# Inverse denominators of a linear attention: spread by ScalarE copies and turned by TensorE, in place of a masked VectorE spread and fp32 products

## The reference, cut to what matters

```python
kv = jnp.einsum('bshd,bshe->bhde', k, v)
ksum = k.sum(axis=1)
vsum = v.sum(axis=1)
num = jnp.einsum('bshd,bhde->bshe', q, kv) * scale + vsum[:, None, :, :]
den = jnp.einsum('bshd,bhd->bsh', q, ksum) * scale + seq_len
return num / den[..., None]
...
o = mala_attn(q, k, v) + lepe_conv(v, lepe_w, lepe_b)
o = o.reshape(Bb, Ss, H * DV) * o_gate
return o @ Wo.T
```

## Time and profile before

| | |
|---|---|
| median of 3 runs | 889.64 us (878.7, 889.64, 890.82) |
| profiled execution | 872.31 us, its span 870.5 us |
| mean granted TensorE clock | 0.953 of full speed |
| TensorE matmul busy | 767.5 us, 88% |
| TensorE weight load busy | 601.0 us, 69% |
| VectorE, ScalarE, GpSimd busy | 474.5, 397.1, 410.5 us |

### The profile page before, as it was taken

One profiled execution on the slowest core, in us unless ns is written; L12 is line 12 of the kernel. 1 busy time (PEld: TensorE's weight loads), 2 busy tenths in 40 slices (PEclk: granted clock), 3 DMA queues, 4 the chain that ended last, 5 costly groups with the idle time before them and its releaser, 6 DMA issues.

```text
span 870.5 us, 13265 instructions
## 1 busy us (share of the span) xinstructions
PE 767.5 (88%) x4302; PEld 601.0 (69%) x4302; DVE 474.5 (55%) x1207; ACT 397.1 (46%) x943; POOL 410.5 (47%) x420
## 2 busy tenths in 40 slices
PE   5999999998888976799888898889999999999963
PEld 4666576575475644478787797888989988997421
DVE  3687788787489415334333343343444444445986
ACT  5585638644442622035445353544456555563000
POOL 0000002666657667456566566555556555666100
PEclk9999999999988978799899999999999999999996
DMA  9500010242248955435565765555565555568795
GB/s 329 165 1 0 1 49 37 99 162 114 113 176 302 356 206 215 140 136 188 176 209 174 247 202 195 178 184 172 172 207 186 168 187 189 184 204 337 279 413 226
DMA packets 82605, 158.45 MB, mean 182 GB/s; under 512 B 14430, under 2 KB 55523, under 8 KB 82280
## 3 DMA queue, kind: packets, MB, share of 16 engines
q1 hardware_dynamic: 58344, 96.74, 33.8%
q0 software_dynamic: 19968, 56.67, 16.5%
q10 hardware_dynamic: 4224, 4.19, 1.4%
HBM read 88.15 MB, written 73.57 MB: 186 GB/s over the span
## 4 chain that ended last, share of the span: by engine, by line
PE 65%; DVE 9%; ACT 8%; issue 7%; another core or an unknown queue 5%; DMA 3%; SPq 2%; ACTq 1%; DVEq 0%
PE ps_wide L1333 15%; PE ps_wide L1348 8%; PE ps_kv L1333 7%; PE ps_narrow L1321 5%; PE ps_wide L1093 5%; PE ps_wide L969 3%; PE ps_narrow L1106 2%; DMA arena<-expert_outs 2%; PE ps_wide L1115 2%; PE ps_wide L1101 2%; PE ps_kv L1115 2%; ACT arena L900 1%; PE ps_narrow L1045 1%; PE ps_wide L1086 1%
## 5 line engine op out<-in xcount | busy, mean ns | idle before, releaser
L544 POOL DMA_INDIRECT expert_rows<-arena,slot_i x192 | 192.5, 1003 | 239.4 <-DVE arena L1649 143.3
L650 POOL DMA_INDIRECT expert_outs<-arena,meta x224 | 217.8, 972 | 158.7 <-DVE arena L1854 106.9
L900 ACT COPY arena<-arena 128x512 f32 x224 | 127.3, 618 | 189.5 <-remote 95.9
L1854 DVE TENSOR_SCALAR arena<-ps_wide,meta 128x256 f32<-128x256 f32 x224 | 97.9, 479 | 172.8 <-PE ps_wide L1348 99.5
L1333 PE MATMUL ps_wide<-arena 128*128 128x128 f32 x1200 | 154.5, 281 | 13.5 <-ACT arena L883 6.6
L1333 PEld LDWEIGHTS ps_wide<-arena 128*128 128x128 f32 x1200 | 149.3, 196 | 24.2 <-ACT arena L883 11.6
L1348 PE MATMUL ps_wide<-arena 128*128 x448 | 117.9, 386 | 1.6 <-issue 1.6
L1348 PEld LDWEIGHTS ps_wide<-arena 128*128 128x128 f32 x448 | 77.8, 194 | 9.2 <-issue 3.1
L1333 PEld LDWEIGHTS ps_kv<-arena 128*128 128x128 f32 x592 | 72.4, 194 | 12.5 <-ACT arena L883 6.4
L1333 PE MATMUL ps_kv<-arena 128*128 128x128 f32 x592 | 74.7, 278 | 7.2 <-issue 3.5
L1093 PE MATMUL ps_wide<-arena 128*128 128x512 f32 x160 | 71.8, 594 | 2.8 <-DVE arena L1545 2.8
(11 more groups left out here) (235 smaller groups left out, 1046.6 us busy)
## 6 DMA issues: line engine op xcount, KB each, us to landing
arena<-expert_rows SPq DMA_DIRECT2D x224, 160.0 KB, 2.8
arena<-expert_outs SPq DMA_DIRECT2D x48, 512.0 KB, 15.8
arena<-w_experts SPq DMA_DIRECT2D x32, 384.0 KB
expert_rows<-pad_row SPq DMA_DIRECT2D x33, 160.0 KB
out<-x ACTq DMA_DIRECT2D x8, 512.0 KB, 10.2
expert_outs<-arena,meta POOLq DMA_INDIRECT x224
x<-x SPq DMA_DIRECT2D x3, 1024.0 KB, 11.0
h_cols<-arena SPq DMA_DIRECT2D x6, 512.0 KB
```

Source lines behind the costliest of these rows:

```text
L544: nc.gpsimd.indirect_dma_start(rows, bass.IndirectOffsetOnAxis(ap=slots_i[b % 2][:, t, k:k + 1], axis=0), hrows[b % 2][:, t, :], None, bou ...
L650: nc.gpsimd.indirect_dma_start(outs, bass.IndirectOffsetOnAxis(ap=meta_i[:, j % METAS, 1:2], axis=0), yb[j % OUTS], None, bounds_check=las ...
L900: last = nc.scalar.copy(wgu[:, j % 4:j % 4 + 1, :], wall[:, bass.ds(expert[j], 1), 0:DOWN])
L1854: v.tensor_scalar(yb[j % OUTS], ps_wide[:, 1, p % 2, j % DUO * D:(j % DUO + 1) * D], meta[:, j % METAS, 0:1], None, ALU.mult).then_inc(s_y ...
```

## The change

The denominators are inverted where they are, with tokens on the partitions. ScalarE then copies each inverse into 32 neighbouring columns (`expand(0)` and `expand(1)`, one instruction of 128 x 1024 for each half, its input read with a step of zero), which gives `rden_x` the layout [token, tile, feature]. `broadcast(hf)` is now eight transpositions of 128 x 128, straight into the PSUM banks that the products wrote. `spread_rden` on VectorE, the one transposition L1268, the semaphore `s_rdt`, the constants `head_rows` and `tile_mask` and the zeroing of `rden` go; the load of `cst` shrinks from 524 to 260 columns; `rden_x` now lies over the whole place of `h2`. The order on TensorE changes: `numerator(1, 1)` and `broadcast(0)` come right behind `turn_rows(2)`, in round 0 `broadcast(1)` also ahead of the gate's projection, in later rounds `turn_next(0)` behind `broadcast(1)`. On ScalarE the two copies stand behind `copy_num(0)` and ahead of `copy_rows(2)` and `copy_num(1)`.

```diff
-        rden_x = take(TILES, P, overlay=h2_at + TILES * D // 2, rows_=TILES * H)
+        rden_x = take(TILES, D, overlay=h2_at)
...
-        PROJ_LOADS = [(cst[:], consts), (wq, w_q), (wk, w_k)]
+        PROJ_LOADS = [(cst[:], consts[:, 0:2 * P + HC]), (wq, w_q), (wk, w_k)]
...
+                def expand(hf):
+
+                    act.wait_ge(s_rden, b + 1)
+                    heads = slice(hf * TPH * H, (hf + 1) * TPH * H)
+                    nc.scalar.copy(rden_x[:, hf * TPH:(hf + 1) * TPH, :].rearrange("p t (h n) -> p (t h) n", n=DK),
+                                   rden[:, heads, None].to_broadcast([P, TPH * H, DK])).then_inc(s_rdx, 1)
...
                 if front and back:
                     act.wait_ge(s_vsum, b + 1)
                     copy_num(0)
+                if front:
+                    expand(0)
+                    expand(1)
                 if back:
                     copy_rows(2)
...
                 def broadcast(hf):
-                    for m in range(C):
-                        last = mm(ps_wide[:, hf, m], head_rows[:, m * P:(m + 1) * P],
-                                  rden_x[:, hf * TPH:(hf + 1) * TPH, :], start=True, stop=True)
+                    pe.wait_ge(s_rdx, b * HALVES + hf + 1)
+                    for i in range(TPH):
+                        for m in range(C):
+                            last = nc.tensor.transpose(ps_wide[:, hf, m, i * P:(i + 1) * P],
+                                                       rden_x[:, hf * TPH + i, m * P:(m + 1) * P], ident)
                     last.then_inc(s_rdb, 1)
...
                         turn_rows(2)
+                    numerator(1, 1)
+                    broadcast(0)
                     if first:
-                        numerator(1, 1)
-                    pe.wait_ge(s_rden, b + 1)
-                    nc.tensor.transpose(ps_wide[:, 0, 1, 0:P], rden, ident).then_inc(s_rdt, 1)
-                    if first:
+                        pe.wait_ge(s_numc, 1)
+                        broadcast(1)
                         pe.wait_ge(s_bcol, 2)
...
                     if back:
-                        numerator(1, 1)
                         turn_rows(3)
-                    if follows and back:
-                        turn_next(0)
-                    pe.wait_ge(s_rdx, b + 1)
-                    broadcast(0)
-                    pe.wait_ge(s_numc, b * HALVES + 1)
-                    broadcast(1)
+                        pe.wait_ge(s_numc, b * HALVES + 1)
+                        broadcast(1)
+                        if follows:
+                            turn_next(0)
...
-                def spread_rden():
-
-                    dve.wait_ge(s_rdt, b + 1)
-                    v.tensor_tensor(rden_x, ps_wide[0:TILES * H, 0, 1:2, 0:P].to_broadcast([TILES * H, TILES, P]),
-                                    tile_mask[:, :, None].to_broadcast([TILES * H, TILES, P]), ALU.mult).then_inc(s_rdx, 1)
```

More of the change, by code:

```diff
@@ L107, in adaln_block_kernel @@
         mod_row = sb("mod_row", [P, B, 2, D])
-        cst = sb("cst", [P, 2 * P + HC + D + TILES])
+        cst = sb("cst", [P, 2 * P + HC])
         ident = cst[:, 0:P]
@@ L111, in adaln_block_kernel @@
         den_mask = cst[:, 2 * P:2 * P + HC]
-        head_rows = cst[0:TILES * H, 2 * P + HC:2 * P + HC + D]
-        tile_mask = cst[0:TILES * H, 2 * P + HC + D:2 * P + HC + D + TILES]
         rcst = sb("rcst", [P, 2 * P + E + TILES + BLOCKS + 1])
@@ L190, in adaln_block_kernel @@
         ksm = take(C, HC)
-        rden = take(P)
+        rden = take(TILES * H)
         wo_g = take(C, D)
@@ L307, in adaln_block_kernel @@
         s_den, s_rden = sem("s_den_summed"), sem("s_rden")
-        s_rdt, s_rdx = sem("s_rden_turned"), sem("s_rden_spread")
+        s_rdx = sem("s_rden_spread")
         s_num, s_numc = sem("s_num_summed"), sem("s_num_copied")
@@ L1217, in body @@
                     shared_down(0)
-                    pe.wait_ge(s_rdx, b)
                     pe.wait_ge(s_taken, b)
@@ L1476, in _ @@
             v.memset(score[:, :, E:E + 2], SENTINEL).then_inc(s_slot, 1)
-            v.memset(rden, 0.0).then_inc(s_taken, 1)
-            v.memset(vt[:, :, 0:PAD], 0.0)
+            v.memset(vt[:, :, 0:PAD], 0.0).then_inc(s_taken, 1)
             v.memset(vt[:, :, PAD + S:PAD + S + PAD], 0.0)
@@ L1672, in invert_den @@
                     dve.wait_ge(s_den, b + 1)
-                    den = rden[:, 0:TILES * H]
-                    link(v.tensor_scalar(den, ps_wide[:, 0, 0, 0:TILES * H], float(S), None, ALU.add))
-                    v.reciprocal(den, den).then_inc(s_rden, 1)
-                def spread_rden():
-                    dve.wait_ge(s_rdt, b + 1)
-                    v.tensor_tensor(rden_x, ps_wide[0:TILES * H, 0, 1:2, 0:P].to_broadcast([TILES * H, TILES, P]),
-                                    tile_mask[:, :, None].to_broadcast([TILES * H, TILES, P]), ALU.mult).then_inc(s_rdx, 1)
+                    link(v.tensor_scalar(rden, ps_wide[:, 0, 0, 0:TILES * H], float(S), None, ALU.add))
+                    v.reciprocal(rden, rden).then_inc(s_rden, 1)
                 def close_o(hf):
@@ L1729, in body @@
                     invert_den()
-                    spread_rden()
                     convolve(range(3, TAPS))
```

## The result

The changed kernel took 886.88 us (median of 6 runs, 884.17 to 893.37), the kernel before, run beside it, 881.07 (6 runs, 865.76 to 890.82): ratio 1.015 [1.01, 1.02], within 2%, but on the other side of my forecast of 878.0. The ratio compares only the runs within 1.5% of each kernel's fastest, and the kernel before spreads over 3%, so I give medians of all runs beside it: 0.66% slower here. The profiled execution took 885.21 us (span 883.4, mean granted clock 0.942) against 872.31 (870.5, 0.953): 12.9 us more, where I had worked out 6.2 less.

What follows compares the result with a forecast made beforehand. The prediction took VectorE's list ahead of closing `o`, not TensorE, to bound each round's end. Gains of 1.35 + 1.9 + 1.46 + 1.52 = 6.2 us gave 866.1 us profiled and 878.0 us as median, range 866 to 893.

Steps and rivals of the forecast that it cites:

- the passing on: Rounds 0 to 3 and what follows: each round's gain was taken to carry forward through the chain, 6.2 us in all.
- 1.35 + 1.9 + 1.46 + 1.52: Gains in us forecast for the closing of `o` in rounds 0, 1, 2 and 3, summed to 6.2.
- Round 1: Close of `o` in round 1: slots follow the ranks at once, TensorE's transpositions end in time; 1.9 us gained.
- Copies: ScalarE's two new copies of 128 x 1024 per round: 1.05 us each, nothing charged for the step of zero.
- Transpositions: TensorE's 16 new transpositions of 128 x 128 per round: 1.1 us for each eight, 2.2 us together.
- From the start of `take_ranks` to L1685: VectorE ahead of closing `o`: 0.87 for ranks plus 1.92 for slots, 2.79 us remaining, in rounds 2 and 3.
- The whole: All four rounds: 6.2 us off the total, 6.4 with copies at nothing, 1.6 with copies of 2.1 us.
- Round 0: Close of `o` in round 0: ready at 69.8 against 71.15, limited by `turn_next(0)` and its turns; 1.35 us gained.
- Rival 2: `project_out(0)`: TensorE's clock falls after sparse transpositions, rounds 0 to 2 lose 8.3 us, net 2.1 us slower; chance 0.17.
- Rival 1: Stalls without a releaser, round 3 and before 361.87, end at their own time; gain 1.5 us or nothing; chance 0.25.
- The sign that I had named for this rival: First expert block: should come some 6 us before 382; if it did not, swallowed gains were the case.
- The spread: Four executions of the kernel before, 872.31 to 890.82 us: said to differ by three times what the change moves.

Runs made afterwards that it cites:

- e5: Changed kernel, nothing edited, on a chip with late signals: 879.58 us, against 875.02 for the shared runs of the kernel before.
- e11: Changed kernel, nothing edited, run again beside three variants: 888.73 us, ratio 1.0089, against 881.48 for the kernel before.
- e16: Changed kernel with every tile back at its address in the kernel before, repeated on another chip: 884.92 us, ratio 1.0019 to the kernel before.
- e6: Kernel before, nothing edited, built again on the chip of e5: 871.22 us, against 875.02 for the shared runs of the kernel before.
- e1: Changed kernel with every tile back at its address in the kernel before: 793.91 us, ratio 0.9944, against 797.34 for the kernel before.
- e12: Changed kernel with 12 spare transpositions on TensorE ahead of the first numerator of rounds 1 to 3, repeating e9: 875.69 us, ratio 0.994 to the kernel before.
- e13: Kernel before with the same 12 spare transpositions ahead of the first numerator of rounds 1 to 3: 880.28 us, ratio 0.9977 to the kernel before.
- e2: Kernel before with its tiles at the changed kernel's addresses: 799.44 us, ratio 0.9999, against 797.34 for the kernel before.
- e7: Changed kernel with batch 0's 48 row scatters held until after round 2's second output projection: 928.55 us in all, kernel before 874.34; read only up to round 2's first.
- e15: Kernel before with VectorE's mask of the kv product done three times in rounds 1 to 3: 900.82 us, ratio 1.019, against 882.03 unedited.
- e9: Changed kernel with 12 spare transpositions on TensorE ahead of the first numerator in rounds 1 to 3: 867.25 us, ratio 1.0003; kernel before 874.34.
- e4: Kernel before with two extra one-column ScalarE copies behind copy_num(0) in each round: 798.79 us, ratio 1.0002, against 797.34 unedited.
- e8: Kernel before with the same 48 row scatters held back as in e7: 939.65 us in all, unedited 874.34; read only up to round 2's first output projection.

## Why the prediction was wrong

**The failed step is the passing on.** I summed 1.35 + 1.9 + 1.46 + 1.52 as if whatever round 1 gains stood in round 2 too, looked for dangers only between the last numerator and `project_out(0)`, and so put TensorE's clock at the numerators at nothing without a reason. Round 1's gain did reach round 2: ScalarE's copy of the gate came at 180.79 against 183.13. It was lost from 187 on. Before, VectorE was busy with its routing until 187.26 and went straight on to the mask. After, it was through at 184.9, stood waiting until 185.49, and TensorE behind it idled for 2.00 us instead of 1.39. Then the clock fell: 16 us at 0.57, 6.9 us of work at full speed, of which 3.4 us reached `project_out(0)` (from -2.42 to +1.02).

All four profiles of the changed kernel on chips with late signals have this long fall in round 2 (the first, e5, e11 and, with the old addresses, e16), and neither of the kernel before has it (the first, e6). That it follows from *more* idle time than before is shown less well. In e5 VectorE went straight from its routing to the mask (185.15) and TensorE idled 1.41 us, much as before the change, and the fall came; in e6 TensorE idled 1.81 us and it didn't.

**The terms themselves** held. Copies: 1.04 us by the median of eight, against 1.05. Transpositions: 1.04 us for eight. Round 1: 137.94 - 71.15 = 66.79 us against 135.52 - 70.69 = 64.83, so 1.96 us, forecast 1.9, with the same short fall at 126 to 130 in both. From the start of `take_ranks` to L1685 it took 2.89 us in rounds 1 and 2 of e1, where I had 2.79. The whole: 6.5 us at equal clock but 3.4 as measured on the quiet chip (e1), 4.6 us with both kernels kept busy (e12, e13), forecast 6.2. Round 0 was mis-sized, 0.46 for 1.35: TensorE idled for 1.25 us until the first copy, the clock dipped (0.89 over 56 to 72), and 16 transpositions took 3.33 us, not 2.2.

**Rival 2** had the right mechanism and side, and nearly the size by that rule, +2.1 us against the +2.13 of round 3's `project_out(0)`; but on the chips with late signals not the place. The long fall of round 2 begins at the first numerators, where the change has edited nothing, and `project_out(0)` itself took 3.70 us in rounds 1 and 2, and in round 3 5.19 against the 6.48 of the earlier trace rows, so that the agreement of 2.1 with 2.13 is luck. On the quiet chip it had the place too: 5.38 us in rounds 1 and 2 of e1 against 3.70 in e2, so 1.7 us in each, of which round 3 gave 1.3 back (5.37 against 6.65). I gave it 0.17 since I looked for too little *density* of TensorE's work, not for idle time handed on from a round before. Its ground from the Trainium skill (TensorE: Matmul & The Clock Gate, "Part 4: PE-mode transpose") was that transpositions don't count as products do and don't bring the full clock. The first half is not borne out here: 12 of them in the idle time kept the clock up (granted 0.57 without them in e11, 0.98 with them in e12). Whether transpositions alone can bring it back after a fall, no run shows.

**Rival 1**, gains swallowed by stalls without a releaser, is the other half: where the scatters are held back (e7), the stalls are gone, the idle time is 0.40 us and there is no long fall. But they do not end at a time of their own, as I had it; they follow TensorE. The copy of the gate comes 7.32 to 7.41 us after the copy ahead of it in every profile with late signals, wherever round 2 stands (at 180.79 in the changed kernel, 183.13 before), and the mask follows its product by 2.05 us in the changed kernel and by 1.87 in e6, both from a wait without a releaser. The sign that I had named for this rival, the first expert block not earlier than 382, came true (385.75), but 2.13 of the 4.25 us of delay stand at round 3's `project_out(0)` already.

**The spread.** I took the spread of executions, three times what the change moves, as noise around a fixed gain. It is mostly the clock: 0.01 of its mean is 7.1 us on the quiet chip. On the chip of e5 the changed kernel's mean clock was 0.938 against 0.948, worth 5.9 us at that chip's slope of 5.9 (+- 1.0) us, and at equal clock it had no gain left (+0.2 +- 1.6). The same reckoning gives +2.3 (+- 1.6) for e11 and -1.3 (+- 1.3) for e16. So on these chips the clock explains the loss against the kernel before, within these errors, but not why the 6.2 us are missing at equal clock; perhaps it is the idle time that late signals leave, but no run shows it. What remains open beside that: why signals are late on the other chips and not on the quiet one, and what decides, beside its length, whether idle time at this place is followed by a long fall: e5 fell after 1.41 us, while there was none after 1.39 and 1.81 us in the kernel before, 2.00 us in round 1 of e15 and 2.41 in round 3 of e16. Lengthening it can bring the fall (rounds 2 and 3 of e15), and filling it is a cure (e9, e12). The changed kernel itself never met the quiet chip; e1 stands for it there, which e2 makes fair.

## What to carry to other kernels

Time gained in one stretch is not passed on by itself: ask at each later wait, where the change has edited nothing too, what had been hiding a late signal, and whether the engine at the end of that wait is the one with a clock to lose. Where runs of one kernel spread by more than the change moves, set time against mean granted clock first: the slope tells which part of a difference is the clock's. And where TensorE has to wait ahead of a dense stretch, some spare transpositions in the gap can be worth more than the optimization that opened it (13.0 us here).

## What was not expected of the hardware

- The kernel before takes 797.34 us on one chip and, by medians, 871 to 890 on the others. On those, signals of TensorE reach ScalarE, VectorE and GpSimd late, in no trace before round 2, at whose start GpSimd's scatters begin, and for the first time at the gate's copy of that round: 7.39 us in place of 5.61. In the expert loop of e11, ScalarE's copies (L908) alone stood 135.1 us in such waits and VectorE's weighting 114.9 (from the listing of waits: engine, tile, line, total, times, longest):

```profile
ACT arena L908 <- remote: 135.1, 39, 7.0
DVE arena L1850 <- remote: 114.9, 40, 5.4
```

- The falls of the clock to half level differ in length: 3.4 us in all over 126 to 131 in the kernel before, 6.8 over 276 to 284, and 13.7 over 187 to 202 in the changed one. The kernel before itself has a long one in round 0 in some executions (`project_out(0)` at 77.7 to 78.1 us in e2, e4, e8, e13 and e15) and none in others (71.15, 70.75); the changed kernel has it too (75.84 in e11, 75.51 in e9).
- A ScalarE copy whose source is read with a step of zero costs no more than any other: 1.04 us for 128 x 1024.
